# A 3x3 convolution of 16x16 images taken by pairs of columns, with four transformed inputs in place of three column taps

## The chip, the core and the metric

The kernel runs on one core of one Trainium2 chip. The core has a matrix engine (TensorE, PE in the profile), a vector engine (DVE), a scalar engine (ACT), a general engine (GpSimd, POOL) and a queue engine that issues the DMAs (SyncE, SP). Each engine works through its own list of instructions in the order in which they were written, and semaphores tie the lists together. The metric is device microseconds for one launch, the median of several runs.

## What is computed

Eight images of 256 channels and 16x16 positions go through one hybrid block and then one transformer layer with experts. The part in which the convolution stands:

```python
fw = _to_windows(_ln_c(_dct_rearrange(feat)))      # frequency windows, 8x8 positions
sw = _to_windows(_ln_c(feat))                      # spatial windows
stf = _idct_rearrange(_from_windows(_win_attn(sw, fw, fw, *a1)))
fts = _from_windows(_win_attn(fw, sw, sw, *a2))
y = concatenate([stf, fts], axis=1)
y = einsum('oi,bihw->bohw', c1_w, y) + c1_b        # 512 -> 256 channels
y = conv(y, c2_w, 3x3, 'SAME') + c2_b              # 256 -> 256 channels
y = relu((y - mean) / sqrt(var + EPS) * bn_g + bn_b)   # mean and variance over all images
out = feat + y
```

The rest (an MLP, a causal attention of 16 heads, eight experts with two chosen for each token) follows once the statistics over all eight images are known.

## The kernel before

**Stages.** `build` calls `windows` and then `images`. `windows` computes the block above up to the convolution's output `z` of all eight images, with its statistics `zst`; `images` needs these statistics of all eight, so a barrier stands between the two. The change touches `windows` only.

**Precision.** Every operand of a large product is split into a high and a low f16 part (`yh` and `yl`, `hi` and `lo`), and three products (high by high, low by high, high by low) stand for one. ACT writes the high part with a copy, POOL or DVE subtracts it to get the low part.

**The steps of an image.** Statistics and normalisation (`statistics`, `deviation`, `normalise`), transposes into channels (`to_channels`, then `xh` and `xl`), values (`values`), queries and keys (`queries` with the argument 1, then 0; high parts `qkh` on ACT, low parts `qkl` on DVE), scores (`scores`), then on DVE bias, maximum and shift for two halves, the exponentials on ACT, the transposes of the probabilities on PE (`turn`), their split (`eh` on ACT, `el` on DVE), the weighted sums (`weigh` on PE, `o` on DVE), the transposes of the output (`out_channels`, PE lines 477 and 481), their split (`och` on ACT, `ocl` on DVE), the fused 1x1 product (`project` on PE, `och`/`ocl` by `wfused`), `y` on DVE, its padded f16 parts `yh` (ACT) and `yl` (POOL), the convolution on PE (line 508), its copy `z` on ACT and the statistics of `z` on DVE.

**The order.** `WINDOW_SLOT` is a table written out by hand. In slot k a step with lag -1 works on image k+1, one with lag 0 on image k and one with lag 1 on image k-1. `window_order` unrolls it, and each engine runs the steps that bear its name in that order. So three images are at work in each slot: the scores and the softmax of image k run beside the convolution of image k-1 and the first steps of image k+1. The four PSUM banks of each parity are shared: the convolution of an image writes banks 2 and 3 of its parity, and `queries` with argument 1 of the image two later waits until they have been read.

**The convolution.** For each of two halves of output channels PE runs nine taps by two halves of input channels by three products, 54 matmuls of 256 columns, 108 an image. Tap (dy, dx) reads a 16x16 window of the padded 18x18 image at an offset. The step is cut in three for each half, six pieces of 18 matmuls.

**The weights.** Six chunks of `wconv` (128x768 f32 each) arrive by DMA through two staging tiles (`stage`), three with image 0 and three with image 1; the load of chunk n waits until chunk n-2 is split. ACT takes a chunk's high part, DVE its low part, in line with their other work.

Of the kernel before, what the change touches and what calls it, by code (L numbers as in the profile page):

```python
# [7 lines left out]
TOK = HW * HW  # L8
# [3 lines left out]
WS = 8  # L12
# [6 lines left out]
TAPS = 9  # L19
GROUPS, GH = 4, 4  # L20
# [20 lines left out]
W_CONV = TAPS * 2 * C  # L41
W_SECOND = {"wfc1": 2 * HID, "wfc2": 4 * C, "wqkv": 3 * 2 * C, "wout": 2 * C, "wgate": 2 * EXPERTS,
# [11 lines left out]
def build(nc, a, out):  # L54
# [6 lines left out]
    with keep:  # L61
# [51 lines left out]
        with first:  # L113
            for name, n in {**W_FIRST, "wconv": W_CONV, "wfused": 2 * 2 * C}.items():
# [14 lines left out]
    ("act_values", 0, 0), ("dve_statistics", -1), ("pe_values", 0, 0), ("sp_load", 1), ("dve_first", -1),  # L129
    ("pool_deviation", 0), ("sp_first", 1), ("dve_shift", 0, 0), ("dve_bias", 0, 1), ("pe_queries", 0, 1),  # L130
    ("act_values", 0, 1), ("dve_max", 0, 1), ("dve_shift", 0, 1), ("dve_sums", 0), ("act_out", 1), ("pe_values",
    0, 1), ("pe_out", 1), ("act_queries", 0, 1), ("pe_queries", 0, 0), ("dve_turn", 0, 0), ("pool_project", 1),
    ("pe_project", 1), ("act_queries", 0, 0), ("pe_scores", 0, 0), ("pe_dct", -1), ("act_project", 1),
    ("pe_scores", 0, 1), ("pe_conv", 1, 0, 0), ("dve_turn", 0, 1), ("pe_fuse", -1), ("pe_conv", 1, 0, 1),
    ("sp_weights", 1), ("pe_conv", 1, 0, 2), ("dve_turn", 0, 2), ("act_exp", 0, 0), ("act_normalise", -1),
    ("dve_turn", 0, 3), ("dve_channels", -1), ("act_exp", 0, 1), ("pe_conv", 1, 1, 0), ("pe_turn", 0, 0),
    ("act_first", -1), ("act_turn", 0, 0), ("act_turn", 0, 1), ("pe_channels", -1), ("dve_weigh", 0, 0),
    ("act_conv", 1, 0), ("dve_weigh", 0, 1), ("act_fold", -1), ("dve_weights", -1), ("act_turn", 0, 2),
    ("act_turn", 0, 3), ("dve_values", -1, 0), ("pe_fold", -1), ("dve_conv", 1, 0), ("dve_values", -1, 1),
    ("pe_turn", 0, 1), ("dve_conv", 1, 1), ("act_channels", -1), ("dve_out", 0), ("act_weights", -1),  # L140
    ("dve_queries", -1, 1), ("dve_queries", -1, 0), ("pe_conv", 1, 1, 1), ("pe_conv", 1, 1, 2), ("dve_y", 0),
    ("dve_fold", -1), ("act_conv", 1, 1), ("pe_weigh", 0, 0), ("pe_weigh", 0, 1), ("dve_bias", -1, 0),
    ("dve_max", -1, 0), ("pool_weights", 0)]
# [62 lines left out]
def windows(nc, a, k):  # L206
# [12 lines left out]
    with ExitStack() as own:  # L219
# [13 lines left out]
        with ExitStack() as early:  # L233
# [8 lines left out]
        y = one("y", [P, HALVES, TOK])  # L242
        yh, yl = one("yh", [P, HALVES, PAD, PAD], f16), one("yl", [P, HALVES, PAD, PAD], f16)
# [6 lines left out]
         y32_done, yh_done, yl_done, conv_done, z_done) = (  # L250
# [5 lines left out]
                              "conv_done", "z_done"))  # L256
# [7 lines left out]
        minus_done, centre_done = sems("minus_done"), sems("centre_done")  # L264
        pads_set, half_set = sem("pads_set"), sem("half_set")
# [3 lines left out]
        def weight_chunks(p, i):  # L269


            if isinstance(i, int) and i == 0:
                each = CONV_CHUNKS // 2
                for n in range(p * each, (p + 1) * each):
                    cols = slice(n * CONV_CHUNK, (n + 1) * CONV_CHUNK)
                    yield n, n % 2, n // 2, CONV_CHUNK, a["wconv"][:, cols], hi["wconv"][:, cols], lo["wconv"][:, cols]
            else:
# [3 lines left out]
                       k["second"][0][:, cols], k["second"][1][:, cols])  # L281

# [12 lines left out]
        def window_rows(t, oh, wi):  # L295
            return t[:, oh, wi * P:(wi + 1) * P].rearrange("p (j x y) -> p j x y", j=2, x=WS)
# [48 lines left out]
        def _(pe):  # L345
# [64 lines left out]
            def queries(c, at):  # L410
# [3 lines left out]
                if at:  # L414
                    pe.wait_ge(xl_done[p], i + 1)
                    freed(pe, z_done[p], i * 2)
# [80 lines left out]
            def conv(c, oh, third):  # L497

                p, i = step_of(c)
                if c == 0:  # L500
                    pe.wait_ge(weights_split, CONV_CHUNKS // 3 * (third + 1))
                pe.wait_ge(yl_done[p], i * 4 + 4)
                for tap in range(third * 3, third * 3 + 3):
                    dy, dx = divmod(tap, 3)
                    for h in range(HALVES):
                        c0 = (tap * 2 + h) * C + oh * P
                        for n, (w, im) in enumerate([(hi, yh), (lo, yh), (hi, yl)]):
                            last = nc.tensor.matmul(bank(p, 2 + oh)[:, 0:TOK], w["wconv"][:, c0:c0 + P],  # L508
                                                    im[:, h, dy:dy + HW, dx:dx + HW],
                                                    start=(tap, h, n) == (0, 0, 0),  # L510
                                                    stop=(tap, h, n) == (TAPS - 1, HALVES - 1, 2))
                if third == 2:
# [7 lines left out]
        def _(act):  # L520
# [87 lines left out]
            def project(c):  # L608
                p, i = step_of(c)
                behind(act, conv_done, c, 2)  # L610
                act.wait_ge(y32_done[p], i * 2 + 2)
                for oh in range(HALVES):
                    for wi in range(2):
                        nc.scalar.activation(image(yh, oh, wi), window_rows(y, oh, wi), ACT.Copy)\  # L614
                            .then_inc(yh_done[p], 1)

            def conv(c, oh):
# [980 lines left out]
```

## Time and profile before

| | us |
|---|---|
| median of 3 runs | 739.96 (736.93 to 745.4) |
| the profiled execution | 740.04 |
| its span, first to last instruction | 738.3 |
| PE busy / DVE busy / ACT busy / POOL busy | 628.5 / 468.0 / 345.8 / 249.2 |
| from the start to the first bias of image 0 | 39.4 |
| from there to the first bias of image 1 | 39.0 |
| the next six images, bias to bias | 202.1 |
| from the bias of image 7 to the second stage | 48.6 |
| second stage (`images`) | 409.1 |

How to read it: the bias of an image (DVE line 764) is the first instruction after its scores, so the distance from one bias to the next is the time that an image takes in the steady state. The profiler's busy time of PE counts matmuls as pipelined, so what a matmul costs is read from the distance between the starts of two, not from its duration.

### The profile page before, as it was taken

How to read it: one execution, taken by the hardware profiler on the slowest of the kernel's cores; microseconds unless marked ns; L12 is line 12 of the kernel's file. 1: busy time of each engine (PE TensorE's matmuls, PEld its weight loads, DVE VectorE, ACT ScalarE, POOL GpSimd, SP SyncE). 2: the span in 40 equal slices, each digit the busy share in tenths (PEclk: the TensorE clock that was granted, in tenths of full speed). 3: DMA queues.
4: the chain of work that ended last, by engine and by line, in shares of the span. 5: the costliest groups of instructions: out<-in, count | busy, mean ns of one | idle time of the engine just before them, and what ended most of it. 6: DMA issues, size and time to landing. Idle time of an engine off the chain costs nothing.

```text
span 738.3 us, 20284 instructions
## 1 busy us (share of the span) xinstructions
PE 628.5 (85%) x8800; PEld 528.7 (72%) x8800; DVE 468.0 (63%) x1032; ACT 345.8 (47%) x548; POOL 249.2 (34%) x260
## 2 busy tenths in 40 slices
PE   5848999999999999574897868898989898988857
PEld 4637787888878788453685646687878787877755
DVE  2577777686777778313364544587768686867445
ACT  4444455463737373106895325544444535361610
POOL 1010203112130303014587427373636454543430
PEclk9868999999999999885798978899999999999997
DMA  7203001010110000001033031221313040400000
GB/s 279 80 1 128 17 3 54 3 54 21 37 40 3 2 3 2 1 29 43 30 72 72 1 72 32 43 57 31 64 25 72 16 73 16 73 16 1 16 16 15
DMA packets 16889, 29.78 MB, mean 40 GB/s; under 512 B 1952, under 2 KB 10400, under 8 KB 15904
## 3 DMA queue, kind: packets, MB, share of 16 engines
q1 hardware_dynamic: 16800, 28.49, 15.4%
q8 instruction: 69, 1.13, 0.6%
q14 instruction: 20, 0.16, 0.1%
HBM read 22.19 MB, written 6.29 MB: 39 GB/s over the span
## 4 chain that ended last, share of the span: by engine, by line
PE 35%; DVE 9%; ACT 5%; POOL 3%; issue 2%; DVEq 0%; POOLq 0%; ACTq 0%
PE ps L201 20%; DVE mx L1391 3%; PE ps L1123 3%; PE ps L1075 3%; PE ps L1101 2%; PE ps L1104 2%; PE ps L986 2%; PE ps L1078 1%; PE ps L1107 1%; DVE acc L1481 1%; DVE st L1333 1%; ACT wide L1211 1%; POOL hl L1297 1%; ACT prob L1240 1%; ACT wide L1201 1%
## 5 line engine op out<-in xcount | busy, mean ns | idle before, releaser
L1311 POOL TENSOR_TENSOR e2l<-prob,e2h 128x1536 f16<-128x1536 f32 x32 | 98.7, 3104 | 16.8 <-ACT e2h L1246 16.8
L201 PE MATMUL ps<-secondh,ch_moe 128*128 128x256 f16 (+1 forms) x320 | 82.5, 265 | 3.4 <-DVE cl_moe L1344 3.1
L508 PE MATMUL ps<-yh,wconvh 128*128 128x256 f16 x288 | 80.4, 279 | 4.2 <-POOL yl L665 4.2
L201 PE MATMUL ps<-secondh,cl_moe 128*128 128x256 f16 (+1 forms) x320 | 82.8, 265 | 0.0
L201 PE MATMUL ps<-secondl,ch_moe 128*128 128x256 f16 (+1 forms) x320 | 82.7, 265 | 0.0
L665 POOL TENSOR_TENSOR yl<-y,yh 128x128 f16<-128x128 f32 x32 | 13.1, 445 | 200.3 <-ACT yh L614 200.3
L508 PE MATMUL ps<-yh,wconvl 128*128 128x256 f16 x288 | 80.5, 279 | 0.0
L508 PE MATMUL ps<-yl,wconvh 128*128 128x256 f16 x288 | 80.2, 278 | 0.0
L1391 DVE TENSOR_REDUCE mx<-ps 128x2 f32<-128x512 f32 (+1 forms) x96 | 65.5, 682 | 22.3 <-PE ps L1078 22.3
L1240 ACT ACTIVATE prob<-ps 128x1536 f32<-128x1536 f32 x32 | 46.4, 1451 | 44.8 <-PE ps L1107 44.8
L1481 DVE SCALAR_TENSOR_TENSOR acc<-ps,gate,acc 128x256 f32<-128x256 f32 x112 | 49.0, 480 | 27.4 <-PE ps L201 27.4
L1075 PE MATMUL ps<-ks,qs 80*128 80x128 f16 (+1 forms) x256 | 38.8, 255 | 17.3 <-DVE mx L1391 17.3
L1246 ACT ACTIVATE e2h<-prob 128x1536 f16<-128x1536 f32 x32 | 47.2, 1477 | 5.2 <-PE ps L1123 4.2
L594 ACT ACTIVATE prob<-prob 128x1024 f32<-128x1024 f32 x16 | 16.9, 1058 | 63.9 <-DVE prob L780 63.9
L1275 POOL TENSOR_TENSOR rstd<-mv,eps 128x2 f32<-128x2 f32 x24 | 4.7, 196 | 117.6 <-DVE mv L1338 117.6
L1075 PEld LDWEIGHTS ps<-ks,qs 80*128 80x128 f16 x256 | 18.9, 100 | 30.1 <-DVE mx L1391 27.4
L1162 ACT ACTIVATE ch_moe<-ps 128x512 f16<-128x512 f32 x16 | 9.5, 596 | 64.5 <-PE ps L201 56.1
L1101 PE MATMUL ps<-qs,ks 80*128 80x256 f16 (+1 forms) x256 | 38.0, 251 | 1.9 <-ACT prob L1240 1.6
L201 PE MATMUL ps<-xh,wqkh 128*128 128x256 f16 x128 | 36.3, 283 | 2.2 <-DVE vl L740 2.1
L201 PEld LDWEIGHTS ps<-secondh,ch_moe 128*128 128x128 f16 x320 | 31.1, 99 | 9.5 <-DVE cl_moe L1344 3.8
L1104 PE MATMUL ps<-shift,headb 128*128 128x256 bf16 (+1 forms) x256 | 37.8, 250 | 0.0
L201 PE MATMUL ps<-xh,wqkl 128*128 128x256 f16 x128 | 36.2, 283 | 0.2 <-issue 0.2
(221 smaller groups left out, 2086.6 us busy)
## 6 DMA issues: line engine op xcount, KB each, us to landing
weights_stage<-in_second SPq DMA_DIRECT2D x6, 684.0 KB, 4.1
qs<-rope_scratch SPq DMA_DIRECT2D x24, 128.0 KB, 3.7
ks<-rope_scratch SPq DMA_DIRECT2D x24, 128.0 KB, 5.5
weights_stage<-in_wconv SPq DMA_DIRECT2D x6, 384.0 KB, 4.3
xw<-in_xw SPq DMA_DIRECT2D x8, 256.0 KB, 2.8
xc<-in_xc SPq DMA_DIRECT2D x8, 256.0 KB, 2.6
rope_scratch<-rh SPq DMA_DIRECT2D x8, 256.0 KB, 2.3
rope_scratch<-rl SPq DMA_DIRECT2D x8, 256.0 KB, 2.3
```

Of the source, the lines that this page charges most:

```text
L201: last = nc.tensor.matmul(out_ap, lhs[x], rhs[w], start=done == 0, stop=done == n - 1)
L508: last = nc.tensor.matmul(bank(p, 2 + oh)[:, 0:TOK], w["wconv"][:, c0:c0 + P], im[:, h, dy:dy + HW, dx:dx + HW], start=(tap, h, n) == (0, ...
L594: nc.scalar.activation(e, e, ACT.Exp).then_inc(exp_done[p], 1)
L1075: nc.tensor.matmul(to[:, m * keys:(m + 1) * keys], qs[p][:, gr * GH + h, q0:q0 + P], ks[p][:, gr * GH + h, 0:keys], start=m == 0, stop=False)
L1101: nc.tensor.matmul(to[:, n * width:(n + 1) * width], ks[p][:, gr * GH + h, k0:k0 + P], qs[p][:, gr * GH + h, q0:TOK], start=n == 0, stop=F ...
L1104: nc.tensor.matmul(to[:, n * width:(n + 1) * width], headb[:, gr * GH + h, :], shift[p][:, q0:TOK], start=False, stop=False)
L1123: last = nc.tensor.matmul(bank(0, 3)[:, c0:c0 + w], e[n % 2][:, e0:e0 + P], v[c % 3][:, kt, gr * GH + h, 0:w], start=(kt, m) == (0, 0), st ...
L1240: nc.scalar.activation(prob[n % 2][:], bank(0, 0, 3), ACT.Exp, scale=SOFTMAX_SCALE).then_inc(exp2, 1)
L1246: nc.scalar.activation(eh[n % 2][:], prob[n % 2][:], ACT.Copy).then_inc(e2_hi, 1)
L1311: nc.gpsimd.tensor_tensor(el[n % 2][:], prob[n % 2][:], eh[n % 2][:], ALU.subtract).then_inc(e2_lo, 1)
L1391: nc.vector.tensor_reduce(mx[c % 2][:, q0 // P, h0:h0 + len(heads)], bank(1, 1).rearrange("p (h m) -> p h m", m=keys), op=ALU.max, axis=AX ...
L1481: nc.vector.scalar_tensor_tensor(acc[c % 2][:, t, :], back_bank(e)[:, t * C:(t + 1) * C], gate[:, t, e:e + 1], (t3 if e == 0 else acc[c % ...
```

## The change

The convolution is taken by pairs of output columns. With d0 to d3 four neighbouring columns of the padded image and g0 to g2 the three taps of a row, it forms d0-d2, d1+d2, d2-d1 and d1-d3 and the weights g0, (g0+g1+g2)/2, (g0-g1+g2)/2 and g2. Four products m0 to m3 give the two output columns: m0+m1+m2 and m1-m2-m3. Each product has 16 rows by 8 pairs, 128 columns, and there are 3 rows by 4 kinds by 2 halves of input by 2 halves of output by 3 products, 144 matmuls of 128 columns an image. Around them:

- `y` is written by DVE straight into the padded f32 image, in four pieces of 128 columns; the padding is now zeroed in `y`.
- POOL forms the four inputs (`turned_y`), per half of the channels one operation of 288 elements and two of 144. ACT writes their high part, 576 elements a half, and a scaled f32 copy of the same size in place; POOL subtracts (576 elements a half).
- After the convolution ACT copies kinds 1 and 2 out of PSUM (`inner`), POOL forms their sum and difference (`mixed`), and DVE adds kind 0 and subtracts kind 3, writing the even and the odd columns of `z` (two operations of 256 elements). The statistics of `z` stay.
- Each weight chunk is now a (row, half) triple of taps. POOL makes the sum, the difference and the total in the staging tile, ACT takes two high parts of 512 columns, DVE two low parts of 512. The convolution's first piece waits for all six chunks.
- `WINDOW_SLOT` is a new table.

```diff
-            def conv(c, oh, third):
+            def conv(c, h, oh):
                 p, i = step_of(c)
                 if c == 0:
-                    pe.wait_ge(weights_split, CONV_CHUNKS // 3 * (third + 1))
-                pe.wait_ge(yl_done[p], i * 4 + 4)
...
+                    pe.wait_ge(weights_split, CONV_CHUNKS)
+                pe.wait_ge(yl_done[p], i * 2 + h + 1)
+                for dy in range(ROWS):
+                    for k in range(KINDS):
+                        c0 = ((dy * 2 + h) * KINDS + k) * C + oh * P
                         for n, (w, im) in enumerate([(hi, yh), (lo, yh), (hi, yl)]):
...
+                            last = nc.tensor.matmul(
+                                kind_bank(p, oh, k), w["wconv"][:, c0:c0 + P],
+                                im[:, k, h, dy:dy + HW, :].rearrange("p r u -> p (r u)"),
...
-            def project(c):
+            def project(c, h):
                 p, i = step_of(c)
                 behind(act, conv_done, c, 2)
...
+                act.wait_ge(pairs_done[p], i * 6 + h * 3 + 3)
+                nc.scalar.activation(yh[:, :, h], turned_y[:, :, h], ACT.Copy, scale=YS / (S * S)).then_inc(yh_done[p], 1)
+                nc.scalar.activation(turned_y[:, :, h], turned_y[:, :, h], ACT.Copy, scale=YS / (S * S))                    .then_inc(y_scaled[p], 1)
+
+            def conv(c):
+
+                p, i = step_of(c)
+                behind(act, mixed_done, c, 2)
+                act.wait_ge(conv_done[p], i * 2 + 2)
                 for oh in range(HALVES):
...
+                    nc.scalar.activation(inner[:, 0, oh, :], kind_bank(p, oh, 1), ACT.Identity,
+                                         scale=1.0 / (S * YS), bias=col("c2b", oh)).then_inc(inner_done[p], 1)
+                nc.scalar.activation(inner[:, 1], kind_banks(p, 2), ACT.Copy,
+                                     scale=1.0 / (S * YS)).then_inc(inner_done[p], 1)
...
+            def pairs(c, h):
+
+                p, i = step_of(c)
+                behind(pool, y_scaled, c, 2)
+                behind(pool, yl_done, c, 2)
+                pool.wait_ge(y32_done[p], i * 4 + 4)
+                near = y[:, h].rearrange("p r (u e) -> p e r u", e=2)
+                nc.gpsimd.tensor_tensor(turned_y[:, 0:4:3, h], near[:, :, :, 0:PAIRS], near[:, :, :, 1:PAIRS + 1],
+                                        ALU.subtract).then_inc(pairs_done[p], 1)
+                odd, even = y[:, h, :, 1:2 * PAIRS:2], y[:, h, :, 2:2 * PAIRS + 1:2]
+                nc.gpsimd.tensor_tensor(turned_y[:, 1, h], odd, even, ALU.add).then_inc(pairs_done[p], 1)
+                nc.gpsimd.tensor_tensor(turned_y[:, 2, h], even, odd, ALU.subtract).then_inc(pairs_done[p], 1)
...
+                for n, op in enumerate((ALU.add, ALU.subtract)):
+                    nc.gpsimd.tensor_tensor(mixed[:, n], inner[:, 0], inner[:, 1], op).then_inc(mixed_done[p], 1)
...
+                        nc.gpsimd.tensor_tensor(total, taps[0], taps[2], ALU.add).then_inc(taps_added, 1)
+                        pool.wait_ge(taps_added, n + 1)
+                        nc.gpsimd.tensor_tensor(other, total, taps[1], ALU.subtract).then_inc(taps_ready, 1)
+                        pool.wait_ge(taps_ready, n * 2 + 1)
+                        nc.gpsimd.tensor_tensor(total, total, taps[1], ALU.add).then_inc(taps_ready, 1)
+                        continue
...
+            def conv(c, par):
+
+                p, i = step_of(c)
+                dve.wait_ge(mixed_done[p], i * 2 + par + 1)
+                halves_of = z[:, :, c * TOK + par:(c + 1) * TOK:2]
+                nc.vector.scalar_tensor_tensor(halves_of, kind_banks(p, 3 * par), (1.0 - 2.0 * par) / (S * YS),
+                                               mixed[:, par], ALU.mult, ALU.add).then_inc(z_ready[p], 1)
```

How the table moves DVE's steps, at two places of a slot. Between the split of the attention output (`ocl`) of one image and the scores of the next, before:

```order
L817 TENSOR_TENSOR ocl<-ps,och 128x1024
L752 SCALAR_TENSOR_TENSOR qkl<-ps,sbqk,qkh 128x256 x8
L824 SCALAR_TENSOR_TENSOR y<-ps,ybias 128x256 x2
L764 SCALAR_TENSOR_TENSOR prob<-ps,relb 128x512 x2
L773 TENSOR_REDUCE mx<-prob 128x16
L722 BN_STATS st<-xw 128x6 x2
L722 BN_STATS st<-ps 128x6 x2
L728 BN_AGGR mv<-st 128x2 x4
L780 TENSOR_TENSOR prob<-prob,mx 128x1024
```

The same place, DVE with the change:

```order
L884 TENSOR_TENSOR ocl<-ps,och 128x1024
L892 TENSOR_TENSOR y<-ps,ybias 128x2x8x8 x4
L819 SCALAR_TENSOR_TENSOR qkl<-ps,sbqk,qkh 128x256 x4
L919 BN_STATS zst<-z 128x6 x2
L819 SCALAR_TENSOR_TENSOR qkl<-ps,sbqk,qkh 128x256 x4
L789 BN_STATS st<-xw 128x6 x2
L789 BN_STATS st<-ps 128x6 x2
L795 BN_AGGR mv<-st 128x2 x4
L831 SCALAR_TENSOR_TENSOR prob<-ps,relb 128x512 x2
L840 TENSOR_REDUCE mx<-prob 128x16
L831 SCALAR_TENSOR_TENSOR prob<-ps,relb 128x512 x2
```

`y` now stands ahead of all eight low parts of the queries (`qkl`) of the next image; the statistics of `z` stand between them, and the statistics of the image after that (`st`, `mv`) stand ahead of the bias in place of behind the first maximum.

ACT's list at the start, from the fused weights to the first exponential, before (`wconvh` are the high parts of the convolution's weights):

```order
L539 ACTIVATE wfusedh<-wf 128x1024
L562 ACTIVATE affine<-ps,vec 128x256 x4
L568 ACTIVATE xh<-affine 128x1024
L627 ACTIVATE wconvh<-weights_stage 128x768 x3
L575 ACTIVATE vh<-ps 128x2x4x32 x4
L586 ACTIVATE qkh<-ps,sbqk 128x256 x8
L594 ACTIVATE prob<-prob 128x1024
```

ACT at the same place with the change:

```order
L571 ACTIVATE wfusedh<-wf 128x1024
L607 ACTIVATE vh<-ps 128x2x4x32 x4
L663 ACTIVATE wconvh<-weights_stage 128x2x256
L666 ACTIVATE wconvh<-weights_stage 128x512
L663 ACTIVATE wconvh<-weights_stage 128x2x256
L666 ACTIVATE wconvh<-weights_stage 128x512
L663 ACTIVATE wconvh<-weights_stage 128x2x256
L666 ACTIVATE wconvh<-weights_stage 128x512
L618 ACTIVATE qkh<-ps,sbqk 128x256 x8
```

The three chunks stood ahead of the values' high parts (`vh`) and now stand behind them, directly ahead of the high parts of the queries (`qkh`).

On PE the pieces of the convolution of image k-1 stand in a slot like this. Before: scores, dct, scores, four pieces (72 matmuls), turn, channels, turn, two pieces (36), weigh, values, queries 1, values, output, queries 0, project. With the change: dct, scores, two pieces (72 matmuls, of 128 columns), turn, channels, turn, one piece (36), weigh, one piece (36), values, values, output, queries 1, project, queries 0.

## Rows read from the trace of the kernel before

**Rows 1.** Windows: stage, length, busy (count) of PE PEld DVE ACT POOL, PEclk, DMA.

```profile
39.41:78.41 39.00, 25.54 (x498) 21.84 (x499) 27.77 (x49) 17.44 (x35) 4.03 (x8) 0.76 0.19 62
...
146.10:179.60 33.50, 32.69 (x606) 28.03 (x605) 25.61 (x48) 18.34 (x36) 7.01 (x12) 1.00 0.11 32
...
280.60:329.20 48.60, 36.81 (x364) 30.18 (x364) 19.47 (x29) 7.94 (x15) 6.51 (x10) 0.89 0.00 1
329.20:738.30 409.10, 344.00 (x3920) 286.61 (x3920) 250.52 (x631) 192.68 (x250) 197.13 (x169) 0.92 0.19 40
```

**Rows 2.** Timeline of PE in one period: start, us, engine, line, out<-in, count, idle.

```profile
154.08 1.03 PE L453 MATMUL ps<-cst,prob 128*128 128x128 f32 x8
...
157.40 0.27 PE L508 MATMUL ps<-yh,wconvh 128*128 128x256 f16 x1
...
161.58 0.20 PE L467 MATMUL ps<-vh,eh 64*128 64x64 f16 x2
...
163.09 0.24 PE L201 MATMUL ps<-wvh,xh 128*64 128x128 f16 x1
...
169.37 1.16 PE L477 MATMUL ps<-cst,o 128*128 128x128 f32 x8
...
170.80 0.27 PE L201 MATMUL ps<-xh,wqkh 128*128 128x256 f16 x1
...
173.42 0.27 PE L201 MATMUL ps<-och,wfusedh 128*128 128x256 f16 x1
...
176.53 0.22 PE L440 MATMUL ps<-qkh 32*64 32x64 f16 x4 [0.33 <-DVE qkl L752]
...
177.43 1.13 PE L382 MATMUL ps<-xw,cst 128*128 128x256 f32 x4
```

**Rows 3.** Timeline of DVE in the same period.

```profile
154.03 1.23 DVE L780 TENSOR_TENSOR prob<-prob,mx 128x1024 f32<-128x1024 f32 x1
156.38 2.29 DVE L788 TENSOR_REDUCE sums<-prob 128x32 f32<-128x2048 f32 x1 [1.12 <-ACT prob L594]
...
158.97 2.42 DVE L795 TENSOR_TENSOR el<-ps,eh 128x512 f16<-128x512 f32 x4
...
162.82 3.59 DVE L808 TENSOR_TENSOR o<-ps,rs 64x256 f32<-64x256 f32 x8
...
172.12 1.23 DVE L817 TENSOR_TENSOR ocl<-ps,och 128x1024 f16<-128x1024 f32 x1 [0.80 <-ACT och L606]
173.26 3.22 DVE L752 SCALAR_TENSOR_TENSOR qkl<-ps,sbqk,qkh 128x256 f16<-128x256 f32 x8
176.39 0.74 DVE L824 SCALAR_TENSOR_TENSOR y<-ps,ybias 128x256 f32<-128x256 f32 x2
179.61 1.29 DVE L764 SCALAR_TENSOR_TENSOR prob<-ps,relb 128x512 f32<-128x512 f32 x2 [2.47 <-PE ps L440]
```

**Rows 4.** Timeline of PE in the second stage: four matmuls of 128 columns, then the next.

```profile
452.38 0.39 PE L1104 MATMUL ps<-shift,headb 128*128 128x128 bf16 x4
452.60 0.38 PE L1107 MATMUL ps<-laterb,identb 128*128 128x512 bf16 x1
```

**Rows 5.** Group of POOL, by form: busy us, mean ns | idle before.

```profile
L1301 POOL TENSOR_TENSOR rot<-rot,turned 128x1024 f32<-128x1024 f32 x8 | 19.3, 2414 | 20.3 <-DVE turned L1377 20.3
```

**Rows 6.** Timeline of ACT: the third weight chunk, values of image 0, an exponential.

```profile
26.85 0.84 ACT L627 ACTIVATE wconvh<-weights_stage 128x768 f16<-128x768 f32 x1 [4.65 <-DMA weights_stage<-in_wconv]
...
30.43 0.66 ACT L575 ACTIVATE vh<-ps 128x256 f16<-128x256 f32 x2 [2.19 <-PE ps L201]
...
155.29 1.06 ACT L594 ACTIVATE prob<-prob 128x1024 f32<-128x1024 f32 x1
```

**Rows 7.** Timeline of PE: the output transposes of image 7, after an idle stretch.

```profile
300.31 2.08 PE L477 MATMUL ps<-cst,o 128*128 128x128 f32 x8 [3.09 <-DVE o L808]
```

**Rows 8.** Windows of PE alone: stage, length, PE busy (count), PEclk, DMA.

```profile
300.00:304.00 4.00, 2.93 (x12) 0.57 0.00 0
...
654.00:656.00 2.00, 0.51 (x4) 1.00 0.00 0
```

More of the change, by code:

```diff
@@ L19 @@
 TAPS = 9
+ROWS, PAIRS, KINDS = 3, HW // 2, 4
 GROUPS, GH = 4, 4
@@ L660, in project @@
+            def project(c, h):
                 p, i = step_of(c)
                 behind(pool, conv_done, c, 2)
-                for oh in range(HALVES):
-                    for wi in range(2):
-                        pool.wait_ge(yh_done[p], i * 4 + oh * 2 + wi + 1)
-                        nc.gpsimd.tensor_tensor(image(yl, oh, wi), window_rows(y, oh, wi),
-                                                image(yh, oh, wi), ALU.subtract).then_inc(yl_done[p], 1)
-            def weights(c):
-                if c < 2:
-                    return
-                for n, slot, _, width, _, high, low in weight_chunks(*step_of(c)):
+                pool.wait_ge(yh_done[p], i * 2 + h + 1)
+                pool.wait_ge(y_scaled[p], i * 2 + h + 1)
+                nc.gpsimd.tensor_tensor(yl[:, :, h], turned_y[:, :, h], yh[:, :, h], ALU.subtract).then_inc(yl_done[p], 1)
@@ new lines, in conv @@
+            def conv(c):
+                p, i = step_of(c)
+                behind(pool, z_ready, c, 2)
+                pool.wait_ge(inner_done[p], i * 3 + 3)
+                for n, op in enumerate((ALU.add, ALU.subtract)):
+                    nc.gpsimd.tensor_tensor(mixed[:, n], inner[:, 0], inner[:, 1], op).then_inc(mixed_done[p], 1)
+            def weights(c):
+                for n, slot, before, width, _, high, low in weight_chunks(*step_of(c)):
+                    if c < 2:
+                        taps = [stage[slot][:, x * C:(x + 1) * C] for x in range(3)]
+                        total, other = (inner_taps(stage[slot])[:, x * C:(x + 1) * C] for x in range(2))
+                        pool.wait_ge(weights_loaded[slot], before * 16 + 16)
+                        nc.gpsimd.tensor_tensor(total, taps[0], taps[2], ALU.add).then_inc(taps_added, 1)
[4 more added lines that the diff above has]
+                        continue
@@ L677, in weights @@
                     last.then_inc(weights_split, 1)
-            run({"pool_deviation": deviation, "pool_project": project, "pool_weights": weights})
+            run({"pool_deviation": deviation, "pool_pairs": pairs, "pool_project": project, "pool_weights": weights,
+                 "pool_conv": conv})
         @block.vector
@@ L1561, in layouts @@
     c2 = L("c2_w")
-    r["wconv"] = stack([c2[:, :, t // 3, t % 3].T for t in range(TAPS)])
+    taps = np.stack([[halves(c2[:, :, dy, dx].T) for dx in range(3)] for dy in range(3)])
+    r["wconv"] = taps.transpose(2, 0, 3, 1, 4).reshape(P, W_CONV)
     second = {"wfc1": stack([L("fc1_w").T]), "wfc2": stack([L("fc2_w").T])}
```

144 lines of the change are left out of this document (78 added, 66 removed).

## Prediction
> **What bounds the kernel now.** I read the windows first, cut at the first bias of each image. Images 1 to 6 each take about 33.5 us with the matrix clock at full rate, and PE is busy for 32.69 of them, DVE for 25.61, ACT for 18.34, POOL for 7.01 [rows 1]. So PE bounds this stage. The cuts at 78.41 and 280.60 put six images into 202.2 us, 33.7 each [rows 1]. Ahead of them lie 39.4 us until the first bias and 39.0 us for the first period, in which PE is busy for 25.54 only. Behind them lie 48.6 us for the last image alone and 409.1 us for the second stage, which the change doesn't touch [rows 1].
>
> Then the timeline of PE and DVE over one period, 146.1 to 179.6. The convolution is 108 matmuls; 36 of them take 157.40 to 161.58, 4.18 us or 116 ns each [rows 2], so 12.5 us of the 33.5. DVE has gaps: it waits 2.47 us for the scores and 0.80 for `och` [rows 3], and more for the values; 33.5 less 25.6 is 7.9 us of idle or hand-over. DVE and ACT hold one long chain for each image (bias, maximum, shift, exponential, split, sum, `o`, `ocl`, `y`, `qkl`), and the convolution is what PE does meanwhile.
>
> **The change part by part.**
>
> *The matmuls.* 144 of 128 columns. The nearest row with full 128 by 128 weights has four of them in 0.22 us, 55 ns each [rows 4]. Bounds: 55 ns below, 116 ns above (no gain from fewer columns). I take 56: the operand is now a dense run of 128 columns. That is 8.1 us an image in place of 12.5, so PE loses 4.4 us of work and would need about 29 us.
>
> *DVE's additions.* Two sums for `z` of 256 elements, for which `qkl` at 3.22/8 = 0.40 us stands [rows 3]; `y` in four pieces of 128 for 0.74 us in two pieces [rows 3], by size about 1.0. Together 1.1 us: DVE needs 25.6 + 1.1 of busy time, some 27 with the hand-overs.
>
> *ACT's and POOL's additions.* ACT: four copies of 576 elements, about 0.6 each by the exponential's 1.06 for 1024 [rows 6], less four small ones: 1.5 us on 18.3, hidden in its idle time. POOL at 2414/1024 = 2.4 ns an element [rows 5]: pairs 2 x 576 elements 3.0 us, `yl` 2.8 for 1.8, `mixed` 1.2; about 13 us a period. POOL's part decides when the convolution may start, see below.
>
> *The order.* Now what ends last. I lay out a period of the new lists with the durations of before, from the bias at 0. DVE: bias 1.3, maximum, bias, shift at 1.2 to 1.3 each (1.29 for a bias, 1.23 for a shift, a maximum over as many elements taken alike [rows 3]) to 5.0; exponential 1.06 to 6.1. PE has half the convolution there, 72 x 56 ns = 4.0 us, done at 3.9, and then stands still until 6.2 for the exponential: 2.3 us lost that it didn't lose before. Turn and channels 2.3 us; the second maximum and shift end at 7.4, its exponential at 8.5, second turn 8.6 to 9.6. Then PE runs without a hole: piece 2.0, weighted sums 1.5, piece 2.0 (15.1), both values 3.4, output 1.4 (19.95). The rows are 161.58 to 163.09 for the sums, 163.09 to 169.37 for two values and a queries step (6.28, less 2.62, less hand-overs), 169.37 to 170.80 for the output [rows 2]. DVE reaches the same point by its own work: split until 10.9, sums 2.6, `xl` 1.15, `o` 3.6 to 18.3 [rows 3]. So from here a faster PE would gain nothing: `o` comes at 18.3, where PE is ready at 18.5.
>
> After the output: `och` 1.0 and `ocl` 1.2 on ACT and DVE to 22.4, with queries 1 (2.62 us, [rows 2]) on PE beside them; project 173.42 to about 176.2, 2.8 us, to 25.35. `y` now stands ahead of `qkl` on DVE, so DVE waits there for about 3 us, with `qkl`, the statistics and the scores queued behind it. Then `y` 1.0, `qkl` 1.6, statistics of `z` 0.7, `qkl` 1.6: 30.4. Scores 2.0 us (176.53 to 179.61 less the 1.13 of dct [rows 2, 3]), since dct is moved into PE's wait: 32.4, next bias 32.6. The moved statistics of the next image (2 us) lie under the scores.
>
> So the period is 32.6 in place of 33.7: of the 4.4 us that PE is spared, 3.3 come back as its waits, 2.3 for the exponential and about 1.5 for `qkl`. Six periods: **-6.5 us**. Bounds of this term: 31.5 a period, if hand-overs are shorter than in the rows, and 33.5, if nothing is gained: -13 to -1.
>
> *The chain `y` to convolution.* From `y` at 26.5: pairs of both halves 3.0 (29.5), ACT's two copies of the first half wait for `qkh` and end near 30, `yl` 1.4: 31.3 at the earliest, in time for the convolution at 32.5. Behind it POOL does the deviation of the next image, whose normalisation must end before ACT's exponential at 5.0; it has some 1.5 us to spare. POOL's strided reads have no row. If they cost twice as much the convolution starts 1.5 us late, and the hole of 2.3 us takes that up. So this is priced at nothing.
>
> *The start.* Before, ACT's first two chunks were done by 22.2 and it waited 4.65 us for the third, ahead of the values; the last values came at 30.4 [rows 6]. Now the values come first, about 4.65 us earlier, near 26; then two chunks (2.2 us) and the third, whose load starts when the first is split (28): 4 us of load (32), three POOL operations of 0.65 (34), ACT 0.6. Then `qkh` and `qkl` 3.2 us with the constants of the fused weights between the two halves (about 2.3, one operation like `ocl` and small ones) to 41, and scores at the low clock, some 3 us: bias near 44.6, **+5** on 39.4. In the next period the second three chunks stand behind `ocl` and ahead of `y`: the load (4), POOL (2) and splits delay `y` from 25.5 to about 31.4, and PE is slow after its wait; no convolution is in it. 32.6 + 5.8 + 1.6 for the low clock gives 40, **+1** on 39.0. Bounds for both together: +3 to +9.
>
> *The end.* Image 7 has no neighbour. Its output's transposes started 300.31 - 280.60 = 19.7 us after its bias [rows 1, 7]; now DVE is done with `o` after 10.9 + 2.6 + 3.6 = 17.1: -2.6. Between `y` and the convolution the pairs add 3.0 us, of which the coarser copies and subtractions give back some 0.6: +2.4. The last convolution starts cold; with the first 4 us at half rate it took about 12.5 + 2 us and takes 8.1 + 2: -4.4. The way out, `inner` 1.1, `mixed` 0.65, `z` 2 x 0.5, statistics 0.7, in place of one copy and one statistics step of 0.4 each, is 2.8 longer. **-1.8**.
>
> Sum: 5 + 1 - 6.5 - 1.8 = -2.3 on the profiled 740.04, so **738**. The profiled execution lies at the median of the three runs (739.96), so the forecast stands for both.
>
> **The rivals.**
>
> *A. No cost at the start, shorter chains.* The third chunk may land while the values are still computed, and DVE's chain may lose some of its hand-overs: start and first period +3, period 32.0 (-10), end -1.8: 731. For it: the new table has the statistics and dct in waits. Against it: the load can't start before the first chunk is split, and ACT reaches that only behind the values.
>
> *B. The clock falls in the new holes.* PE stands still for 2.3 us each period and then does only 3.3 us of transposes around a further wait. After an idle 3.09 us the granted clock was 0.57 in the 4 us window and eight transposes took 2.08 us for 1.16 [rows 7, 8]. If it falls once a period, turn, channels and a piece lose 1.5 to 2 us: +9 to +12, some 748. [...] Against it: at 654 PE had 0.51 us of work in 2 us and the clock stayed at 1.00 [rows 8].
>
> *C. Weight loads bound the short matmuls.* Each needs its own 128 columns of weights. Taken at 85 ns, the middle of the bounds, the first 72 still fit ahead of the exponential (6.1 us), the other 72 cost 2.1 us a period and the end 3: +15.6, 754: slower than before. Rows 4 speak against it with 55 ns. The Trainium skill, TensorE: Matmul & The Clock Gate, section Back-to-back issue gap, gives about 81 ns for a pair of weight load and matmul at 128 columns; by that figure the kernel would take about 752, and this case's trace disagrees.
>
> *D. POOL is late.* If `pairs` and `yl` together cost more than twice my price, `yl` ends over 2.3 us after the scores and every further us is paid six times: 745 with 1 us.
>
> **How the numbers follow.** Forecast (733 to 746) 0.55; A 0.20; B 0.13; C 0.06; D 0.06. For faster by over 1% (below 732.6, what a measurement here can tell from no change) about half of A and its tail plus the lower edge of the forecast's term for the period: 0.23. Slower by over 1% (over 747.4): C, half of B, some of D and of a start worse than +9: 0.20. Same 0.57. The range 729 to 750 leaves out C, part of A's tail and of B.
>
> **What would show it.** The matmuls of the convolution start 56 ns apart. PE shows two new waits each period, about 2.3 us ahead of the first turn, on the exponential, and 1.5 ahead of the scores, on `qkl`; DVE shows about 3 us ahead of `y`. The distance between first biases is 32.6 from image 1 on; the first lies near 44.6, the second near 84.6. The granted clock stays at 1.00 between them. It is wrong if the biases are under 31.5 or over 33.5 apart, if a hole drops the clock, or if the first bias comes before 42.

## The result, and the profile after

The changed kernel takes 748.52 us (median of 4 runs, 747.83 to 752.37), the kernel before 740.36 beside it (736.93 to 745.4). The ratio is 1.0133, 95% interval 1.0082 to 1.0185: slower by about 1.3%, clear of the noise, where 738 was forecast. The profiled execution's span is 746.7 us, 8.4 more than the 738.3 of before.

The windows of the changed kernel, cut at first biases as in [rows 1] (stage, length, busy time and count of PE, PEld, DVE, ACT and POOL, PEclk, DMA share, GB/s):

```profile
42.80:84.05 41.25, 23.43 (x499) 21.51 (x500) 29.23 (x54) 20.11 (x39) 12.46 (x21) 0.75 0.10 35
84.05:293.70 209.65, 178.26 (x3838) 164.55 (x3837) 157.00 (x304) 120.70 (x222) 67.70 (x99) 0.93 0.07 24
153.60:188.80 35.20, 30.20 (x643) 28.00 (x642) 26.45 (x52) 20.57 (x39) 11.82 (x18) 0.93 0.09 30
293.70:746.70 453.00, 371.01 (x4356) 312.78 (x4354) 271.27 (x666) 202.16 (x267) 205.44 (x181) 0.91 0.17 36
```

Four differences make up the 8.4 us. The first bias comes at 42.8 in place of 39.41: +3.4. The first period is 41.25 in place of 39.0: +2.2. The next six periods are 209.65 in place of 202.1 (34.9 each, not 32.6): +7.5. From the last bias to the end it is 453.0 in place of 457.7: -4.7.

The periods are where the forecast fell. The waits of PE in the seven periods, from 79 to 300 us (engine, what waits, released by: us in total, times, longest), first before, then after:

```profile
PE ps L440 <- issue: 3.3, 3, 1.3
PE ps L440 <- DVE qkl L752: 2.0, 6, 0.3
```

```profile
PE ps L472 <- issue: 16.3, 7, 2.7
PE ps L472 <- DVE qkl L819: 15.1, 7, 6.2
PE ps L485 <- ACT prob L626: 6.4, 10, 1.1
PE ps L509 <- DVE o L875: 1.3, 6, 0.2
```

L440 and L472 are the scores. The waits on `qkl` and on the exponential were foretold. The first line was not: 16.3 us, in all seven images, in which PE stands in the middle of the scores and no semaphore that the profile shows holds it ("issue"). The timeline of PE shows the scores of one image (start, us, engine, line, operands, count, idle before); the last line is the first matmul of the convolution:

```profile
184.05 0.22 PE L472 MATMUL ps<-qkh 32*64 32x64 f16 x4 [1.35 <-DVE qkl L819]
...
185.20 0.22 PE L472 MATMUL ps<-qkh,qkl 32*64 32x64 f16 x4
185.23 0.20 PE L472 MATMUL ps<-qkl,qkh 32*64 32x64 f16 x2
188.12 0.21 PE L472 MATMUL ps<-qkl,qkh 32*64 32x64 f16 x2 [2.68 <-issue]
...
188.64 0.23 PE L539 MATMUL ps<-yh,wconvh 128*128 128x128 f16 x1
```

142 of the 192 matmuls are done in 1.4 us, then PE gets nothing for 2.68, then the other 50 run. The next bias waits for them. In the eight images the hole is 1.57 to 2.72 us long and lies 136 to 153 matmuls into the scores. Before, five of the eight images have one, four of 0.90 to 1.27 us (images 1, 2, 5 and 6, at 153, 183, 154 and 187 matmuls) and one of 0.17 in image 0 (at 140), and I had taken the scores' 2.0 us from an image that had none [rows 2].

What comes in there? The queues of the page (packets, MB, share), after and before:

```profile
q8 instruction: 71, 1.16, 0.7%
```

```profile
q8 instruction: 69, 1.13, 0.6%
```

The page counts 9088 matmuls and as many weight loads after, 8800 before. 2 x 9088 / 256 is exactly 71.0 and 2 x 8800 / 256 is 68.75: one packet (16 KB) carries about 256 of PE's instructions, that is 128 matmuls with their loads. The transfers in the window from 182 to 190 us:

```profile
DMA  0000000000000000002000000000000000000020
...
q8 instruction: 2, 0.03, 1.4%
```

The stretch is cut into 40 slices of 0.2 us: one packet comes near 185.7, as PE runs dry, the other near 189.6. PE goes on 2.4 us behind the first; what fills that time the profile doesn't show. The memory is otherwise idle in the hole: from 185.5 to 188.1 the DMA share is 0.02, and the granted clock is 1.00.

The place of the holes says more. Number PE's matmuls in the trace from the start of the program. In the changed kernel PE stands ahead of number 348, 857, 1492, 2129, 2766, 3403, 4040 and 4677, in the kernel before ahead of 348, 857, 1491, 3274 and 3911. The first three are the same to within one, and the last two of before lie 129 ahead of 3403 and 4040. From the third on the numbers of the changed kernel are 637 apart, five times 127.4: the holes follow a count of instructions.

### The profile page after: what moved, and what is told of

It reads as the page before. It is cut to its first block, busy times and chain, and to the rows that moved or that the text cites. A ratio compares the mean times of both kernels' runs of the same rounds, so it can differ in the third digit from the quotient of the medians.

```text
span 746.7 us, 21018 instructions
## 1 busy us (share of the span) xinstructions
PE 599.7 (80%) x9088; PEld 521.2 (70%) x9088; DVE 477.2 (64%) x1070; ACT 362.5 (49%) x562; POOL 297.9 (40%) x325
## 4 chain that ended last, share of the span: by engine, by line
PE 34%; DVE 9%; ACT 5%; POOL 3%; issue 2%; DVEq 0%; POOLq 0%; ACTq 0%
PE ps L203 20%; DVE mx L1470 3%; PE ps L1202 3%; PE ps L1154 3%; PE ps L1180 2%; PE ps L1183 2%; PE ps L1065 2%; PE ps L1157 1%; PE ps L1186 1%; DVE acc L1560 1%; DVE st L1412 1%; ACT wide L1290 1%; POOL hl L1376 1%; ACT prob L1319 1%; ACT wide L1280 1%
## 5 line engine op out<-in xcount | busy, mean ns | idle before, releaser
L1390 POOL TENSOR_TENSOR e2l<-prob,e2h 128x1536 f16<-128x1536 f32 x32 | 98.7, 3104 | 16.8 <-ACT e2h L1325 16.8
L539 PE MATMUL ps<-yh,wconvh 128*128 128x128 f16 x384 | 79.0, 242 | 5.5 <-POOL yl L716 5.5
L539 PE MATMUL ps<-yh,wconvl 128*128 128x128 f16 x384 | 78.8, 242 | 0.0
L539 PE MATMUL ps<-yl,wconvh 128*128 128x128 f16 x384 | 78.4, 241 | 0.0
L724 POOL TENSOR_TENSOR mixed<-inner 128x256 f32<-128x256 f32 x16 | 11.3, 728 | 124.4 <-ACT inner L655 124.4
L539 PEld LDWEIGHTS ps<-yh,wconvh 128*128 128x128 f16 x384 | 42.3, 110 | 6.5 <-POOL yl L716 5.7
L539 PEld LDWEIGHTS ps<-yl,wconvh 128*128 128x128 f16 x384 | 42.6, 111 | 0.0
L539 PEld LDWEIGHTS ps<-yh,wconvl 128*128 128x128 f16 x384 | 42.4, 110 | 0.1
```

Source lines behind the costliest of these rows:

```text
L539: last = nc.tensor.matmul(kind_bank(p, oh, k), w["wconv"][:, c0:c0 + P], im[:, k, h, dy:dy + HW, :].rearrange("p r u -> p (r u)"), start=( ...
L1390: nc.gpsimd.tensor_tensor(el[n % 2][:], prob[n % 2][:], eh[n % 2][:], ALU.subtract).then_inc(e2_lo, 1)
```

## The theory and its rivals

**Block border.** PE's instructions arrive in blocks of 128 matmuls. When PE passes a border the next block is asked for, and that takes some 3 to 4 us. From the matmul 128 ahead of a hole to the end of the hole it is 3.2 to 4.0 us in the changed kernel and 3.3 to 3.7 in the kernel before, and the shortest distance of two of these packets in any run is 3.26 us. In the convolution 128 matmuls take 7 us (56 ns each), and where a whole block lies in it PE shows no such wait. The scores run 128 matmuls in 1.2 us, so PE runs dry if a border lies in their first third. Before, a period has 604 matmuls (the windows' 606 and 643 count some of the neighbour's), 33 short of these 637, so the border moves by 33 matmuls from image to image and lies badly in only some. After, a period has 640: the border moves by 3 only, and it happens to be in the bad place in all eight. Why five blocks are 637 matmuls and not 640 isn't shown; other instructions of PE would do it.

**Rivals.** The moved dct: it stood between the halves of the scores and gave 1.1 us for the refill, and without it every hole could be just what was always there. A busier memory or a lower clock in the new waits: the time would then depend on the work, not on a count of instructions.

## The experiments

**a_shift64, a_shift32.** Spare matmuls of one column, once in the whole program, so that the borders of all later images move. a_shift32 has the first of the two pieces only. spare(n) issues n float32 matmuls of one column of `const("dct")` into an idle bank; the profile counts two records for each, so 16 are 32 matmuls.

```diff
@@ PE, dct(c), behind its last matmul
+                if c == 0:
+                    spare(16)
@@ PE, turn(c, at), ahead of its waits (a_shift64 only)
+                if (c, at) == (0, 0):
+                    spare(16)
```

> The changed kernel with 64 spare one-column matmul records on PE, once, in idle time of image 0 (32 behind the first dct, 32 ahead of its first turn); nothing else moves. Theory (the hole of 2.1 to 2.7 us inside the scores is PE out of instructions: they come in blocks of 128 matmuls with their weight loads, and a period of 642 matmuls is 5 blocks and 2, so that the same border falls 139 to 154 matmuls into the scores of every image): from image 1 on the border moves to 75 to 90 and the next one behind the scores into the convolution, whose slack hides the stall. The hole inside the scores goes, the biases come 32.5 us apart, 735 us. Rival 1 (a late semaphore, or the scores behind one another are slow as such): the hole stays, 748 to 750. Rival 2 (the supply is short on average, wherever the borders lie): the hole stays or moves by no more than a tenth, 748 to 750.

> The changed kernel with 32 spare records behind the first dct only. Theory of the block border: it moves to 107 to 122 matmuls into the scores; the border before it lies 6 to 21 matmuls ahead of them, where PE's list is read on before the wait for the low parts of the queries, so its refill starts earlier than the scores and the hole shrinks to between 0 and 1.5 us: biases 32.6 to 34 us apart, 735 to 744 us. Rivals 1 and 2: the hole stays at 2.1 to 2.7 us, 748 to 750.

Measured: 730.99 us (ratio to before 0.992, 0.989 to 0.995) and 730.6 (0.991, 0.988 to 0.994), both below what was expected. A few spare matmuls took 17.5 us off 748.5, or some 16 by the ratios, since the kernel before took 737.34 beside these runs and 740.36 beside the first. PE's waits in the same stretch, first a_shift64, then a_shift32:

```profile
PE ps L478 <- DVE qkl L827: 15.3, 7, 6.3
PE ps L493 <- ACT prob L634: 8.4, 13, 1.4
PE ps L547 <- issue: 8.2, 6, 1.6
```

```profile
PE ps L493 <- ACT prob L634: 16.0, 12, 2.1
PE ps L478 <- DVE qkl L827: 15.2, 7, 6.2
...
PE ps L547 <- issue: 0.5, 2, 0.3
```

The scores (L478 here) have no hole left. With 64 it lies in the convolution (L547), where the wait for the exponential covers it; with 32 it is gone but for 0.5 us, and the wait for the exponential is the 16 us over 7 images, 2.3 each, that the prediction gave. Its periods are 32.1 to 33.1, 195.12 us for six (in a_shift64 192.82). The holes of images 2 to 7 were 14.8 us, and these six periods are 14.5 and 16.8 shorter. The two windows of a_shift32:

```profile
40.89:81.17 40.28, 23.79 (x498) 21.95 (x499) 29.53 (x54) 20.14 (x38) 13.38 (x21) 0.75 0.11 36
81.17:276.29 195.12, 171.41 (x3838) 158.04 (x3837) 157.08 (x305) 121.13 (x222) 69.06 (x102) 0.97 0.08 26
```

**a_shift96.** 48 and 48 records in the same places: is it their number, or the place of the border?

> The changed kernel with 96 spare one-column matmul records once (48 behind the first image's dct, 48 ahead of its first turn). With 32 and 64 the holes left the scores. Theory of the borders: the border comes back into the scores from behind, 42 to 58 matmuls in, and PE runs dry 170 to 186 matmuls in, for some 2 to 2.7 us, in every image but the first: 744 to 750 us. If spare matmuls help by themselves (a clock kept up, a warmer start), 96 do as well as 64: 729 to 732 us.

Measured: 752.01 us (1.0171, 1.012 to 1.022), 2 above the expected range, with the first bias 2.4 later than in the changed kernel. More spare matmuls brought the holes back:

```profile
PE ps L478 <- issue: 14.9, 7, 2.7
```

They lie 168 to 185 matmuls into the scores, ahead of number 985, 1620, 2257, 2894, 3531, 4168 and 4805: the numbers of the changed kernel in images 1 to 7, each 128 on. So what counts is the place, and a spare matmul does no good by itself.

**a_dct_between, b_dct_first.** dct put back between the halves of the scores in the changed kernel, and taken out from between them in the kernel before, each by one name moved in the table.

```diff
@@ a_dct_between: WINDOW_SLOT of the changed kernel
-  ("pe_dct", -1), ("dve_bias", 0, 0), ("pe_scores", 0, 0), ("act_project", 1, 0), ("pe_scores", 0, 1),
+  ("dve_bias", 0, 0), ("pe_scores", 0, 0), ("act_project", 1, 0), ("pe_dct", -1), ("pe_scores", 0, 1),
@@ b_dct_first: WINDOW_SLOT of the kernel before
-  ("pe_scores", 0, 0), ("pe_dct", -1), ("act_project", 1), ("pe_scores", 0, 1),
+  ("pe_dct", -1), ("pe_scores", 0, 0), ("act_project", 1), ("pe_scores", 0, 1),
```

> The changed kernel with the dct step of the table put back between the two halves of the scores. Theory of the block border: the border stays at 139 to 154, and the 1.1 us of the dct run while the next block is under way, so the hole shrinks by about 1.1 us to 1.0 to 1.6; the scores with the dct take about the same 4.7 us, PE waits 1.1 us longer ahead of them, and the biases stay 34.8 apart or come 0.3 later, since the statistics wait for the dct: 747 to 751 us. Rival 1 in the form that two halves of scores directly behind one another are slow as such (the dct between them is what the kernel before had): the hole goes and a period loses 1.6 us, 739 us.

> The kernel before with the dct step ahead of both halves of the scores, as the new table has it. Theory of the block border: a period of 606 matmuls moves the border by 34 from image to image, so only the images whose border before the last lies 0 to 64 matmuls into the scores get a hole (images 0, 1, 2, 5, 6 as now), and it is longer by the dct's 1.1 us, 2 to 2.6 us; the other images have none. 5 images by 1.1 us, less the dct that now fills PE's short wait: 740 to 746. Rival 1 (halves of scores directly behind one another are slow as such): every image has a hole of 2.1 to 2.7 us, 752 us.

Measured: 750.57 us (1.0181, 1.012 to 1.024) and 742.39 (1.0058, 1.000 to 1.012). The waits on issue in the scores, a_dct_between and b_dct_first:

```profile
PE ps L534 <- DVE qkl L881: 20.5, 7, 7.2
...
PE ps L534 <- issue: 5.3, 5, 1.9
```

```profile
PE ps L499 <- issue: 8.2, 4, 2.2
```

In the kernel before, the holes stay in the same images and grow from 0.9 to 1.3 us to 2.0 to 2.2, by dct's 1.1 us. In the changed kernel they shrink from 16.3 to 5.3 over seven images, 1.6 each and so more than was expected, but dct then takes its time between the halves, PE waits for `qkl` 5.4 us more than in the changed kernel, and the kernel is no faster. So dct's move lengthens the holes and gives about as much back: it doesn't explain the loss.

**b_shift64.** The same 64 records in the kernel before.

> The kernel before with the same 64 spare one-column matmuls that took 17 us off the changed kernel. Theory of the block borders: 606 matmuls a period leave 94 over a multiple of 128, so the border moves by 34 an image whatever the start, and a shift only changes which images have it in the scores: holes of about 1 us in 3 images in place of 5, so -1 to -2 us at most, 736 to 740 us, a ratio of 0.995 to 1.0. If the spare matmuls helped by something else (a clock kept up, a start that they warm), the kernel before would gain some 10 us or more too: 728 or less.

Measured: 743.32 us (1.0044, 1.001 to 1.008). In the periods it went as the theory has it: holes in the scores of three images (3, 4 and 7) in place of five, and two short ones (0.56 and 0.26 us) ahead of the scores, and 240.2 us from the first to the last bias in place of 241.1. All of that gain is in the first period (36.7 for 39.0); the six behind it take 203.5 for 202.1. And the total rose by 3.8 us of span where 1 to 2 less was expected. The first bias is 2.2 us later (41.57), and the second stage, whose code is the same, takes 410.2 us from the first aggregate of `z`'s statistics in place of 407.2. In neither stage does PE have a wait on issue over 0.15 us, so the borders don't explain these 5 us. The granted clock from 420 to 520 us is 0.83, where before it is 0.90; why is open.

**b_lock_bad, b_lock_good.** The kernel before with 34 spare records in every image, so that a period has 638 matmuls, one more than the 637 of five blocks, and the border all but stands still; the second has 48 more once, which put it ahead of the scores.

```diff
@@ PE, conv(c, oh, third), behind its wait
+                if (oh, third) == (0, 0):
+                    for _ in range(17):
+                        nc.tensor.matmul(bank(p, 2)[:, 0:1], const("dct"), const("dct")[:, 0:1], start=True, stop=True)
@@ b_lock_good also: PE, dct(c)
+                if c == 0:
+                    spare(24)
```

> The kernel before with 17 spare one-column float32 matmuls (34 records) ahead of the first convolution piece of every image, in the time in which PE has nothing else that is due. The period is then 640 = 5 x 128 matmuls, so the border of the instruction blocks no longer moves from image to image. Without a shift at the start it stays some 25 matmuls into the scores. Theory of the borders: a hole of 0.9 to 2.3 us in every image from the second or third on (the kernel before has it in 5 of 8), and 741 to 746 us. If the holes have another cause, the kernel keeps its pattern of images with and without them.

> The same kernel with 48 more spare records once, behind the first image's dct. Theory of the borders: the border now stays some 20 matmuls ahead of the scores in every image, no hole in any, all periods near those of the kernel before that have none (33.2 to 33.6): 731 to 736 us, 7 to 10 us less than b_lock_bad, from 24 one-column matmuls in one place. If a fixed border does nothing, both kernels take the same time.

Measured: 795.63 and 786.65 us. Both totals miss, since I priced the 34 records at about 1 us an image and they take 4.4 (198.28 to 202.66), 0.13 each, in a place where PE has no slack. Against each other the two tell what was asked. Waits on issue from 79 to 300 us in b_lock_bad:

```profile
PE ps L444 <- issue: 4.5, 5, 1.2
```

All eight images have the hole (0.64 to 1.89 us), ahead of matmul 348, 857, 1491, 2128, 2765, 3402, 4039 and 4676, each within one of its number in the changed kernel; b_lock_good has none in any, and its list of waits in this stretch holds no issue. 24 one-column matmuls in one place are worth 9.0 us, though they make the first bias 4.6 later. The six periods are 12.1 us shorter, of which 6.4 are holes; from 79 to 300 us the granted clock is 0.95 for 0.92. That a fixed border makes or saves a hole in each image is thus shown on both kernels.

**a32_y_late, a32_start, a32_both.** With the holes gone, can the changed kernel be bettered? The first puts `dve_queries(-1, 1)`, half of the low parts of the next image's queries and keys, ahead of `dve_y` in the table of a_shift32; the second puts the weight splits of images 0 and 1 ahead of the values again; the third does both.

> The changed kernel with the 32 spare one-column matmuls of a_shift32 (730.6 us, period 32.09) and one row of the table moved: DVE makes the low parts of image 1's queries before y and not behind it. In a_shift32 DVE then waits about 3 us for the project matmuls with those parts still to make. If the period is bound by DVE's chain to the scores, it falls by up to the 0.9 us of those parts, to about 31.2, seven periods, -6 us: 724 to 725 us. If the instruction blocks' borders move to the scores again, or POOL or PE bound the period, it stays at 730 to 731.

> a_shift32 with the act and dve transfers of the weights of images 0 and 1 put ahead of the value transfers, as in the kernel before. If the changed kernel's later start (first bias at 42.8 against 39.4; 40.9 in a_shift32) comes from the order of the weight pieces on ACT and DVE, the first bias comes at 39.5 to 40.5 and the time is 728 to 730 us. If it comes from the POOL chain or the weight chunks, no change: 730 to 731 us.

> Both edits of a32_y_late and a32_start in one kernel. Expected the sum of the two: 722 to 725 us, if they act in different stages (start and periods); 730 if neither acts.

Measured: 728.1 us (ratio to before 0.983, 0.977 to 0.990), 731.89 (0.989, 0.982 to 0.995) and 731.53 (0.988, 0.980 to 0.997). None gained what was hoped for, and no total is told from that of a_shift32 (ratio 0.991, 0.988 to 0.994). In a32_y_late the quiet periods are 31.72 in place of 32.09; 0.87 us of low parts went into DVE's wait, but `y` came 0.47 later, since `qkl` waits for ACT's high parts:

```profile
104.66 1.66 DVE L889 SCALAR_TENSOR_TENSOR qkl<-ps,sbqk,qkh 128x256 f16<-128x256 f32 x4 [1.97 <-ACT qkh L688]
106.23 0.87 DVE L962 TENSOR_TENSOR y<-ps,ybias 128x128 f32<-128x128 f32 x4
```

The start edit moved the first bias by nothing (41.16 against 40.89) and made the first period 42.7 in place of 40.3: the order of the weight splits by itself isn't what makes the start of a_shift32 1.5 us later than before. What does stays open.

## Why the prediction was wrong, by its steps

**The step that failed is the scores' term, 2.0 us.** It was a row of an image that happened to have no hole [rows 2, 3], and the lists were laid out as if PE always had its next instruction. Measured: 184.05 to 188.71, 4.7 us, of which 2.7 is the hole, in which PE waits for its next block of instructions. With it the period is 34.9 in place of 32.6, and six periods, forecast at -6.5, were +7.5. Take the border away and the term comes out: in a_shift32 six periods are 195.12, 7.0 less than before. Against the forecast's span of 736.0 (738.3 - 2.3) the measured 746.7 is 10.7 more: +14.0 in the six periods, +1.2 in the first, -1.6 at the start, -2.9 at the end.

**The other steps of the period held.** The 36 matmuls of a piece take 163.32 to 165.43, 2.1 us or 59 ns each with the hand-over to the next group; their starts are 56 ns apart, as forecast:

```profile
163.32 0.22 PE L539 MATMUL ps<-yh,wconvh 128*128 128x128 f16 x1
163.38 0.22 PE L539 MATMUL ps<-yh,wconvl 128*128 128x128 f16 x1
163.44 0.22 PE L539 MATMUL ps<-yl,wconvh 128*128 128x128 f16 x1
...
165.43 0.20 PE L499 MATMUL ps<-vh,eh 64*128 64x64 f16 x2
```

Rival C's weight loads don't bound this. The 81 ns that the Trainium skill, TensorE: Matmul & The Clock Gate, section Back-to-back issue gap, gives for such a pair aren't what this trace shows. The first 72 of an image are slower: 70 to 93 ns apart in images 0 to 6 of the changed kernel, 56 to 67 in a_shift32. The wait for the exponential hides it. DVE in the same period, from a bias at 153.63:

```profile
153.63 1.29 DVE L831 SCALAR_TENSOR_TENSOR prob<-ps,relb 128x512 f32<-128x512 f32 x2 [2.60 <-PE ps L472]
...
168.64 3.58 DVE L875 TENSOR_TENSOR o<-ps,rs 64x256 f32<-64x256 f32 x8
...
175.03 1.23 DVE L884 TENSOR_TENSOR ocl<-ps,och 128x1024 f16<-128x1024 f32 x1 [0.69 <-ACT och L638]
179.33 0.89 DVE L892 TENSOR_TENSOR y<-ps,ybias 128x128 f32<-128x128 f32 x4 [3.08 <-PE ps L203]
...
182.35 1.65 DVE L819 SCALAR_TENSOR_TENSOR qkl<-ps,sbqk,qkh 128x256 f16<-128x256 f32 x4
...
188.85 0.69 DVE L831 SCALAR_TENSOR_TENSOR prob<-ps,relb 128x512 f32<-128x512 f32 x1 [3.02 <-PE ps L472]
```

`o` starts at 15.0 (laid out: 14.7), `y` at 25.7 (25.5) after the foretold wait of 3.08, and `qkl` ends at 30.4 (30.4). Up to the scores the hand-made schedule is right within 0.4 us; the error of this period lies behind it. PE's two new waits came in the foretold size as well: 2.3 us on the exponential in a_shift32, and 1.35 on `qkl` in images 2 to 6, for 2.3 and about 1.5. (These two make 3.8, where the prediction put their sum at 3.3.)

**The start.** +3.4 for +5, and +2.2 for +1. Of the +3.4, 1.7 is the hole in the scores of image 0, for which the forecast had no term; without it, in a_shift32, the first bias comes at 40.89, so the term of +5 measured +1.5. ACT did wait 3.17 us for the third chunk, for the 4 us of the forecast, but a32_start, which undoes that order, gains nothing: the mechanism of this term isn't shown. Of the first period's +2.2, 1 us is the hole (40.28 without it).

**The end.** From the last bias: output transposes after 17.5 us in place of 19.8 (-2.3, forecast -2.6), `y` to convolution +2.3 (+2.4), the convolution itself 9.6 in place of 13.8 (-4.2, forecast -4.4), the way out from the convolution to the aggregate 6.9 in place of 4.0 (+2.9, forecast +2.8), and -0.6 from the transposes to `y`, which had no term. Together -1.9 for -1.8: this term held. The rest of the -4.7 is 2.8 us in the second stage, whose code is unchanged: 404.4 from the first aggregate to the end, in place of 407.2. I had no term for it, and with runs of the kernel before from 736.93 to 745.4 one profile of each doesn't make it an effect of the change.

**The rivals.** A, shorter chains: with the holes gone its sizes come nearest. In a_shift32 and a_shift64 start and first period cost 2.8 and 3.2 us (A: 3), a period is 32.5 and 32.1 on the average (A: 32.0), and the times are 730.6 and 731.0 (A: 731). Its reason for the start isn't borne out, since ACT did wait for the third chunk.

B, the clock: the granted clock is 0.93 over the six periods, where before it is 1.00 over the six and in a_shift32 0.97. The holes cost clock too. Behind the 2.11 us hole of image 3 the scores' matmuls show 0.27 to 0.31 us in place of 0.22, and the convolution's first piece runs at 90 ns:

```profile
152.78 0.27 PE L472 MATMUL ps<-qkh 32*64 32x64 f16 x3 [2.11 <-issue]
...
153.16 0.28 PE L472 MATMUL ps<-qkh,qkl 32*64 32x64 f16 x4
```

That is part of what the shift brings back. B's own mechanism, a foretold wait that drops the clock, is there too, in some periods of a_shift32. Behind the wait for the exponential in image 2 the granted clock is 0.50 from 121.2 to 123.6, and the transposes of `channels` take 1.92 us:

```profile
119.37 1.18 PE L493 MATMUL ps<-cst,prob 128*128 128x128 f32 x8 [2.12 <-ACT prob L634]
120.34 1.92 PE L430 MATMUL ps<-cst,xn 128*128 128x128 f32 x8
```

The three of the six periods with a clock of 0.95 or 0.96 take 32.5 to 33.1 us, the other three, at 0.98 to 1.00, 32.1 to 32.4. In a_shift64 the clock is 1.00 over all six, at 32.1 to 32.4. So this costs up to 1 us in some periods, not 1.5 to 2 in each; why only some have it isn't shown. B's price of 748 is the measured time by chance; its cause isn't the one found. C is answered above. D, POOL late: the changed kernel has no wait on `yl` in the periods.

**What I should have seen.** [rows 1] give about 606 matmuls a period (604 by the trace), and the profile before had five waits on "issue" in L440, 4.3 us together, that appear in some images only. Both were in view. Holes in images 0, 1 and 2, none in 3 and 4, two again in 5 and 6, none in 7: that is what a count modulo something makes.

With the border out of the way the change is worth about 6.5 us: 730.6 and 730.99 against 737.34 for before on the same chip. Some 4 of them are holes that the kernel before has and that the shifted one hasn't; a kernel before without any, at its own price, I haven't got.

## What to carry to other kernels

Look at waits on "issue" inside bursts of very short matmuls. If they come in some iterations only, count PE's instructions per iteration: an edit that makes this number a multiple of the block can turn a hole that was rare into one in every iteration, or into none, and its price (here some 16 us, more than twice the edit's own 6.5) has nothing to do with what the edit computes. Try an edit with two or three instruction counts before you judge it, and take the length of a step from several iterations, not from one.

## What the runs showed of the hardware

Instruction blocks come in packets of 16 KB for 256 instructions: 8800, 9088, 9120 and 9184 matmuls with as many loads made 69, 71, 72 and 72 packets (68.75, 71.0, 71.25 and 71.75 by the quotient, which rounded up is the number in all thirteen profiles). A block takes 3 to 4 us from the passing of the border to PE's going on. PE can outrun them where 128 matmuls take about 1.2 us, and then stands for up to 2.7 us. The Trainium skill, Runtime: NRT & Kernel Launch, section Instruction fetch mechanics, describes refills of this size and calls their cost mostly hidden; where a whole block lies in the convolution the trace agrees, in the scores it doesn't.

A one-column float32 matmul with 128x128 weights took 0.11 us a record where the granted clock was 1.00 (b_lock_good), more than a float16 matmul of 128 columns (56 ns). In a place without slack spare matmuls aren't free.

The second stage, with the same code in all kernels, took from 404.4 to 410.2 us in the thirteen profiles. Before and b_shift64 are the longest. PE has no wait on issue over 0.15 us in it in any of them, so it isn't holes of the kind above.
